# Rotary attention ordered as one sequence of sixteen blocks instead of five groups, with the output products of a key tile in one piece

## What is computed

```python
xn = _layernorm(x, axis=-1)
x = x + _L2_attn_ref(xn, wq, bq, wk, bk, wv, bv, wo, bo) + _L2_ffn_ref(xn, ...)
```

```python
q = (x @ wq + bq).reshape(b, s, H, hd)      # k, v alike with G = 2 heads
q = q * cos + rotate_half(q) * sin           # k alike
scores = jnp.einsum('bqhd,bkhd->bhqk', q, k_exp) * hd ** (-0.5)
attn = jax.nn.softmax(scores, axis=-1)
out = jnp.einsum('bhqk,bkhd->bqhd', attn, v_exp).reshape(b, s, d)
return out @ wo + bo
```

## Time and profile before

| what | us |
|---|---|
| median of 3 runs (5335.07 to 5343.89) | 5343.05 |
| profiled execution | 5337.84 |
| its span, first to last instruction | 5336.0 |
| rotary attention, first row score to last output product | 3268.01 to 3821.1 |
| group 0 / group 2 / group 4 of it | 82.23 / 127.12 / 96.10 |

### The profile page before, as it was taken

How to read it: one execution, slowest core, us unless ns; L and a number is a source line. 1 busy time by engine, 2 the same in 40 slices (tenths; PEclk the granted TensorE clock), 3 DMA queues, 4 the chain that set the end, 5 groups by cost and what they waited for, 6 DMA issues and landing times. The chain is left out here.

```text
span 5336.0 us, 137730 instructions
## 1 busy us (share of the span) xinstructions
PE 5131.5 (96%) x58178; PEld 3403.7 (64%) x58178; DVE 3248.5 (61%) x7450; ACT 2734.7 (51%) x5938; POOL 1909.1 (36%) x2361
## 2 busy tenths in 40 slices
PE   6999999999999989999999999999899999999999
PEld 3666666666666665777777754333366677677555
DVE  6899999999998963444444427666255444444222
ACT  5888888888887841555555411566622222222111
POOL 4889888888888850000000002000000111111000
PEclk8999999999999989999999998999999999999999
DMA  1000000000000000000000000000232111111322
GB/s 32 7 8 9 10 8 8 7 8 8 7 12 25 3 6 13 17 11 13 15 11 11 21 1 16 1 1 1 65 87 80 64 69 69 63 64 69 84 59 53
DMA packets 52286, 149.15 MB, mean 28 GB/s; under 512 B 5593, under 2 KB 10969, under 8 KB 51673
## 3 DMA queue, kind: packets, MB, share of 16 engines
q1 hardware_dynamic: 33600, 105.74, 6.0%
q10 hardware_dynamic: 18072, 34.61, 2.8%
HBM read 103.63 MB, written 2.10 MB: 20 GB/s over the span
## 5 line engine op out<-in xcount | busy, mean ns | idle before, releaser
L719 POOL TENSOR_TENSOR d_kq<-d_kq,d_tot 128x512 f32<-128x512 f32 x448 | 527.6, 1178 | 91.8 <-PE d_lpd L323 66.8
L825 DVE SCALAR_TENSOR_TENSOR d_qkv<-d_fr,d_wts,d_qkv 128x509 f32<-128x509 f32 (+2 forms) x576 | 427.0, 742 | 33.1 <-ACT d_qkv L663 16.0
L2094 DVE TENSOR_REDUCE r_nm<-r_ps 128x2 f32<-128x1024 f32 x256 | 307.7, 1222 | 142.6 <-PE r_ps L1895 142.5
L312 PE MATMUL d_fr<-xnT,d_wts 128*128 128x512 f32 x768 | 371.1, 607 | 11.6 <-DVE d_qkv L825 6.6
L1266 POOL TENSOR_TENSOR f1rstd<-f1var,mhalf 128x4 f32<-128x4 f32 x3 | 3.0, 1011 | 1056.9 <-DVE f1var L1291 1056.9
L2002 ACT ACTIVATE r_pT<-r_ps 128x512 f32<-128x512 f32 x512 | 274.9, 598 | 146.7 <-PE r_ps L1903 146.1
L723 POOL TENSOR_TENSOR d_kF<-d_kF,d_tot 128x256 f32<-128x256 f32 x448 | 307.8, 687 | 116.6 <-PE d_lpd L323 111.7
L1601 DVE TENSOR_TENSOR c_sc<-c_sc,c_mask 128x128 f32<-128x128 f32 x256 | 76.7, 299 | 382.3 <-PE c_sc L1453 382.3
L1498 PEld LDWEIGHTS c_po<-c_pT,c_vt 128*128 128x128 f32 x2304 | 294.7, 191 | 21.0 <-ACT c_pT L1563 9.3
L1498 PE MATMUL c_po<-c_pT,c_vt 128*128 128x128 f32 x2304 | 301.9, 276 | 0.2
L1895 PE MATMUL r_ps<-r_kT,r_qT 32*128 32x512 f32 x1024 | 293.8, 700 | 2.7 <-DVE r_nm L2094 1.1
(11 more groups left out here) (563 smaller groups left out, 13473.3 us busy)
## 6 DMA issues: line engine op xcount, KB each, us to landing
e_wts<-in_w3all SPq DMA_DIRECT2D x42, 897.0 KB
lead<-in_w3all SPq DMA_DIRECT2D x22, 897.0 KB, 4.5
f2wide<-f2gate_rows ACTq DMA_DIRECT2D x64, 256.0 KB
f3wide<-f3gate_rows ACTq DMA_DIRECT2D x40, 256.0 KB
d_wts<-in_headw SPq DMA_DIRECT2D x16, 583.5 KB
c_wqo_more<-in_wqo SPq DMA_DIRECT2D x21, 256.0 KB
f3ws<-in_f3w SPq DMA_DIRECT2D x13, 384.0 KB, 11.2
f2ws<-in_f2s SPq DMA_DIRECT2D x13, 256.0 KB, 8.8
```

What stands on the lines that cost most here:

```text
L312: last = nc.tensor.matmul(fr[:, bank, :], w_of(u)[:, w0 + kd * P:w0 + (kd + 1) * P], T.xnT[:, kd, tok(u):tok(u) + GRP], start=(kd == 0), s ...
L719: return nc.gpsimd.tensor_tensor(v, v, bc(bc(by_pair(u, lv)[:, :, 0], 2, h), 1, 2), ALU.mult)
L825: return nc.vector.scalar_tensor_tensor(into, fr[:, x // 2, 0:GRP - 3 + i], tap(u, x, i), into, ALU.mult, ALU.add)
L2094: nc.vector.tensor_reduce(nm[:, t % 2, half, 4 * j + i0:4 * j + i0 + 2], ps[:, row_pair(row - 1):row_pair(row - 1) + 2], AX, ALU.max).then ...
```

## The change

The five groups become one sequence of 256 row steps. A block is one head group of one group of 512 queries, 16 blocks of 16 steps. The column scores of a step follow the row scores of the same block 22 steps later (`LAG`), and the outputs follow 4 steps behind the columns (`AV_LAG`), so the sequence has 282 steps. Steps 0 to 21 have row scores alone, 22 to 255 both, 256 to 277 column scores alone, and 278 to 281 outputs alone.

```diff
-                for G in range(5):
-                    for s in range(STEPS):
...
+                lg_bank = into_cols()
+                for s in range(STEPS):
+                    c = s - LAG
...
-                        if G in (1, 2, 3) and s >= 4:
-                            outputs(G - 1, s // 2 - 2, s % 2, s % 2)
-                        if G == 4 and s % 2 == 1 and s >= 5:
-                            outputs(G - 1, s // 2 - 2, 0)
-                        if G == 4 and s % 2 == 1 and s < 32:
...
+                    if s < NT:
+                        for kd in range(KD):
+                            last = nc.tensor.matmul(ps[:, lg_bank, s * E2:(s + 1) * E2], T.xnT[:, kd, tok(s)], gw[:, kd], start=(kd == 0), stop=(kd == KD - 1))
...
+                    if turning(s) is not None:
+                        block_transposed(turning(s))
+                    if AV_LAG <= c < ROWS + AV_LAG:
+                        N = (c - AV_LAG) // 2
+                        if s % 2:
+                            outputs(N, 0, 1)
```

The bank plan of the columns is three banks up to step 257 and seven after it; row pairs are two throughout:

```diff
+            next_bank = lambda: 4 + len(col_bank) % 3 if s < ROWS + 2 else len(col_bank) % 7
...
-            if NT <= use < FIRST_ROWS:
-                return 2 * ((use - NT) % 3)
-            return 2 * (use % 2)
+        row_pair = lambda use: 2 * (use % 2)
```

A turn is now of one block (four transposes of four query tiles, one head group), at step 3 of the next block, and the emptying of the pipeline between groups is gone. On ACT the evacuation stands ahead of the exponentials of its step:

```diff
+                    if c % PER == AV_LAG and c >= PER:
+                        evacuate(c // PER - 1)
+                    if 0 <= c < ROWS:
+                        N = c // 2
+                        for w in range(2):
...
-                        if G and s % 16 == 4 and s >= 16:
-                            evacuate(G - 1, s // 16 - 1)
```

More of the change, by code:

```diff
@@ L1824, in heads_transposed, with block_transposed @@
                     last.then_inc(cols_mm, 1)
+                def block_transposed(b):
+                    G, j = divmod(b, 4)
+                    pe.wait_ge(maxed, b + 1)
+                    k = into_cols()
+                    for x in range(4):
+                        last = nc.tensor.transpose(ps[:, k, x * P:(x + 1) * P], qp[:, 4 * G + x, 4 * j:4 * j + 4].rearrange("p h d -> p (h d)"), T.ident[:])
+                    last.then_inc(cols_mm, 1)
                 def keys_transposed(t):
@@ L1885, in finish @@
                         last.then_inc(cols_mm, 1)
[L1887 to L1907, removed]
-                        if G in (1, 2, 3) and s >= 4:
-                            outputs(G - 1, s // 2 - 2, s % 2, s % 2)
-                        if G == 4 and s % 2 == 1 and s >= 5:
-                            outputs(G - 1, s // 2 - 2, 0)
-                        if G == 4 and s % 2 == 1 and s < 32:
-                            t = s // 2
-                            for kd in range(KD):
-                                last = nc.tensor.matmul(ps[:, 6, t * E2:(t + 1) * E2], T.xnT[:, kd, tok(t)], gw[:, kd], start=(kd == 0), stop=(kd == KD - 1))
-                            if t == NT - 1:
-                                last.then_inc(logits_mm, 1)
-                        if G >= 2 and s % 16 in (1, 7, 13):
-                            finish(4 * (G - 2) + s // 16, (s % 16) // 6)
-                    if G < 4:
-                        pe.wait_ge(maxed, 4 * G + 4)
-                        heads_transposed(4 * G + 3)
-                    if G:
-                        outputs(G - 1, 30, 0)
-                        outputs(G - 1, 31, 0)
-                    if G < 4:
-                        pe.wait_ge(cols_read, col)
-                    if G in (0, 3):
-                        pe.wait_ge(rows_read, row)
@@ new lines, in _ @@
+                for s in range(STEPS):
+                    c = s - LAG
+                    if c % PER == AV_LAG and c >= PER:
+                        evacuate(c // PER - 1)
+                    if 0 <= c < ROWS:
+                        N = c // 2
+                        for w in range(2):
+                            i = 2 * (c % 2) + w
+                            k = from_cols()
+                            if i == 0 and N >= 3:
+                                act.wait_ge(av_mm, N - 2)
+                            nc.scalar.activation(pT[:, N % 3, i, :], ps[:, k, :], ACT.Exp).then_inc(cols_read, 1)
+                    if s == NT - 1:
+                        ch = Chain(act, act_steps, 0)
+                        k = from_cols()
+                        nc.scalar.activation(lg[:], ps[:, k, 0:NT * E2].rearrange("p (t e) -> p t e", e=E2), ACT.Copy).then_inc(cols_read, 1)
+                        act.wait_ge(cols_read, lg_slot + 1)
+                        ch.link(nc.scalar.activation(e1[:], lg[:], ACT.Abs))
+                        ch.link(nc.scalar.activation(e1[:], e1[:], ACT.Exp, scale=-1.0))
+                        nc.scalar.activation(e1[:], e1[:], ACT.Ln, bias=T.ones[:, 0:1]).then_inc(softplus_ready, 1)
+                    if s == LAG + 10:
+                        act.wait_ge(less_max, 1)
+                        nc.scalar.activation(p[:], p[:], ACT.Exp).then_inc(exp_ready, 1)
+                    if turning(s) is not None:
+                        turned_queries(turning(s))
+                    if finishing(c):
+                        finish(*finishing(c))
@@ L2110, in _ @@
                             dve.wait_ge(exp_ready, 1)
                             dve.wait_ge(late_loaded, 64)
-                            two_best(nc, ch, E2, p, e1, key, sel, both, top, tot, order, T.w2[:], 1e-20)
+                        two_best(nc, ch, E2, p, e1, key, sel, both, top, tot, order, T.w2[:], 1e-20, parts=(ROUTE_PARTS[s],))
                 for t in range(12, 16):
```

177 lines of the change are left out of this document (89 added, 88 removed).

## The result

The changed kernel takes 5359.80 us, the median of 7 runs (5353.75 to 5366.86), against 5342.56 for 7 runs of the kernel before. The ratio is 1.0033, with a 95% interval of 1.0022 to 1.0045: slower by more than the 0.2% that a measurement can tell, where 5338 and no change had been forecast. The profiled execution took 5356.20 us, 18.4 more than that of before.

What follows compares the result with a forecast made beforehand. PE bounds the kernel, in a loop through PE and ACT over three banks. Head 42.5, pairs 445.1, turns 8.3, finish parts 19.9 and tail 32.0 sum to 547.8 us against 553.1; forecast 5338 us, range 5318 to 5362.

Steps and rivals of the forecast that it cites:

- The pair, 3.87 us: Two steps with both scores and one whole output, looping through three banks: 3.87 us against 3.44 before.
- The rival in which the wait doesn't appear: Last column product finds its bank free: pairs of 3.01 us, 99 us less, 5239; chance 0.06.
- Evacuations: ACT's evacuations of outputs, 28 us of waits before, hidden behind two steps of scores: costed at nothing.
- turns: Between scores and outputs on PE, counted in full: 0.59 us each, 14 in the joint stretch, 8.3 us.
- finish parts: Parts standing in full on PE: ten tiles of 1.93 and one more part 0, 19.9 us in the joint stretch.
- tail: Steps 256 to 281, with seven banks a tile takes 2.07 us; together 32.0 us.
- Joint stretch: Steps 26 to 255, both kinds of scores: 115 pairs of 3.87, 445.1 us, plus 8.3 and 19.9 for extras.
- The rival of cheaper ends: Head at full clock (3.6 us), turns and parts half hidden (14): 17.6 us less, 5320; chance 0.19.
- The clock in the joint stretch: Rival: lone bands let the clock fall to 1.2 GHz, 3.22 us per pair so run, slower; chance 0.15.
- The head: Steps 0 to 25, row scores with logits in the first 16 steps: 42.5 us, from 39 to 48.

Runs made afterwards that it cites:

- e4b: Changed kernel with each exponential over 256 of the 512 queries only, output products reading these twice; 5332.65 us (one run).
- e9: Kernel before with whole outputs behind every second step in groups 1 to 3, instead of halves behind each; 5361.96 us (one run).
- e11b: Changed kernel with two more score products, in the two free bands, in each of the first 16 steps; 5340.69 us (one run).
- e5: Changed kernel with three row pairs in steps 0 to 15, logits left in the head; 5356.13 us (one run).
- e1: Changed kernel with the 64 logit products in one block ahead of step 0; 5350.74 us (11 runs), 1.0011 of before.
- e6: Changed kernel with the logits moved into the joint stretch, two row pairs kept in the head; 5354.45 us (one run).
- e10: Changed kernel with one more whole-array product of 128x512 behind the logits in each of the first 16 steps; 5392.68 us (one run).
- e8: Changed kernel with logits in the joint stretch, three row pairs in steps 0 to 20, and half outputs; 5298.35 us (4 runs), 0.9905 of before.
- e3: Changed kernel with logits in one block ahead of step 0 and outputs in halves; 5314.77 us, 0.9947 of before.
- e7: Changed kernel with logits moved into the joint stretch and three row pairs in steps 0 to 20; 5342.23 us (one run).

## Why the prediction was wrong

**The pair, 3.87 us: right.** Start to start it is 3.87 in the changed kernel, and e4b moved the loop by the 0.21 that its exponential lost. e9 shows the same 3.87 in the old order of blocks. The rival in which the wait doesn't appear is refuted. The rule of the Trainium skill on drains, which the prediction put behind it, says nothing of a bank, and so was no reason for it.

**Evacuations, turns, finish parts, tail: right.** Joint stretch and tail came within 0.8 and 0.1 us. A turn is in full on PE (3446.96 to 3447.55, then the outputs). In the joint stretch an evacuation shows no gap behind it, where the earlier trace rows had one; the outputs around it are 3.87 us apart like all others:

```profile
3364.49 1.07 PE L1870 MATMUL r_out<-r_pT,r_v 128*32 128x512 f32 x8
...
3365.63 0.60 ACT L1980 ACTIVATE r_oT<-r_out 128x512 f32<-128x512 f32 x1 [0.43 <-PE r_out L1870]
...
3368.36 1.06 PE L1870 MATMUL r_out<-r_pT,r_v 128*32 128x512 f32 x8
```

In the tail, where two steps of scores take 1.07 us, the one evacuation before the last (3823.86) does leave PE idle for 0.65, a cost put at nothing; that the tail's sum comes within 0.1 is in part luck. The rival of cheaper ends gets nothing.

**The clock in the joint stretch: the rival did not come.** It is 1.00 for 471 us. The clock fell elsewhere. The prices of this rival are added to the wrong base, 5332.5 instead of the forecast of 5338: one pair in ten would be 5375, not 5370, and the 5362 of the range is about 7 pairs, not 9.

**The head: the step that failed.** The term of 42.5 us took 64.8, 22.3 of the 23.0 us by which the stage missed its sum. Of these, 17.0 are in the 16 steps with logits (46.0 for 29) and 5.3 in steps 16 to 25 (18.8 for 13.5, at 1.2 GHz up to about 3332). The steps themselves were sized rightly: at 2.4 GHz they take 1.60 (step 0) and 1.62 (e11b) where 1.59 was put down. What was wrong is the clock. The prediction saw the right risk: group 0 had a mean granted clock of 0.74, and the same share would have made 34.3 of the 25.4 us. It then took 29, "nearer to the full clock, because PE has more to do". That reason was wrong twice. By the mean it should have been 34, and a mean over group 0 is the wrong row: the two arrangements aren't alike. In group 0 the rows stand alone with three pairs, and its clock goes down and comes back; in the changed head it went down and stayed for 60 us. The trace of before holds both levels, which a cut of group 0 into short stretches would have shown:

```profile
3316.00:3324.00 8.00, 8.00 (x30) 3.35 (x26) 7.53 (x7) 0.00 (x0) 0.00 (x0) 0.50 0.00 0
3324.00:3332.00 8.00, 7.76 (x32) 2.24 (x28) 7.97 (x9) 0.00 (x0) 0.00 (x0) 0.93 0.01 2
```

At 1.2 GHz DVE keeps its pace there, too (7.53 of 8). So group 0 paid little for its low clock, and the price of that clock in the new head, where DVE is not the pace, had to be worked out from the length of its own step: 16 steps at up to 2.97 us, 46.0 in all, where 29 were taken. Had the term been bounded by both levels (25.4 and, as an estimate, twice that, 50.8), its upper end would have been 64.3 for the head, and slower would have had a far larger chance. The fall was foreseen as a rival, but in the joint stretch; it came in the head, where a step's rows use two bands and the logits hold back the rows of the next.

**What stays open.** In the runs here the clock stayed at 1.2 GHz with rows in two bands and logits between (the change, e5), with rows alone on two pairs (e1, e6), and with a whole-array product added (e10). It came back with three pairs and no logits (group 0, e8), and in every kernel by a few us after the first column products of step 22 (in the change at about 3332, 6 us after them; in e3 and e5 about 1 us ahead of them). It did not fall in e11b's 16 steps. That PE is busy is not what decides (e10); what does is not settled by these runs. The opening ahead of the head is the same in all of them, so it alone does not decide either. Nor is it known why e7 kept 2.4 GHz for the first 20 us of the same head in which e8 fell at about 3276. Since two executions of one head can differ so, what e5, e6, e10 and e11b show of the clock, with one execution each, is less firm than the level of the change.

## What to carry to other kernels

Cut the start and end of a stage into stretches of a few us and read the granted clock in each, and price a stretch with part of the array at both levels, 1.2 and 2.4 GHz, before taking a mean from another arrangement. Where banks go round and the engine works in order, the operation between two uses of a bank is cover; before two such operations are merged to save their overhead (0.14 us here), look at what the cover hides (0.57), and at each stretch by itself: in the tail, with banks to spare, the merged outputs save 1.18 us a pair. A third buffer that looks superfluous at the full clock can be what keeps the next engine at its pace at the half clock.

## What was not expected of the hardware

A PE that is busy by the records for all of 72 us (e10), with whole-array float32 products in every step of 4.86 us, was granted 1.2 GHz all the while; twice the row products in the other two bands made the step shorter, 1.62 instead of 2.97 us, and with them the clock stayed at 2.4 GHz (e11b).
